# First unit, block barrier and final gate of an attention and feed-forward kernel on one core

## The chip, the cores and the metric

The kernel runs on one core of a Trainium2 chip. A core has a matmul engine (TensorE, PE in the profile; its weight loads are PEld), a vector engine (VectorE, DVE), a scalar engine (ScalarE, ACT), a general engine (GpSimd, POOL) and a queue engine that issues transfers (SyncE, SP). Each works through its own list of instructions in order and waits on semaphores for the others. The metric is the device time of one execution in microseconds (us); lower is better.

## The reference

```python
xn = _layernorm(x)                      # x: (2, 512, 512), float32
s = _L0_attn_ref(xn, wq, wk, wv, wo)    # 32 query heads, 8 key/value heads of 128, RoPE, window 128
g = _silu(_L0_ffn_ref(xn, ...))         # 512 -> 1792 -> 512, weights (int - zero) * scale
x = x + s * g
```

The attention projects `xn` to q, k and v, rotates q and k by position, takes a softmax over the own block of 128 positions and the one before, weighs v with it and projects out with `wo`. The feed-forward part computes `silu(xn @ gate) * (xn @ up)` and multiplies it by `down`.

## The kernel before

There are 1024 tokens, held as 8 tiles of 128. Products are made in three passes of float32r operands: each operand is split into a rounded part (`hi`, a copy on ACT) and a remainder (`lo`, a subtraction on POOL or DVE), and a product is lo·hi + hi·lo + hi·hi (`three_passes`, L36 to L38). A projection of 128 output rows by 512 tokens is 4 × 3 = 12 matmuls.

`attention_block` has one program for each engine. Work is cut into 16 units, one for each pair of key/value head and batch (`unit = 2 * g + b`); a unit has 7 steps that leave PSUM (`PROJ`): k (k = 0), four q (1 to 4), v (5) and the transposed v (6), in three PSUM banks by turns. Each unit has 4 query blocks j. For one block PE transposes the probabilities (`turn_probs`), computes the scores of the next block (`scores`), projects something of the next unit (`project(..., BEFORE[j])`), projects the finished block before out (`project_out`), weighs the values (`weigh_values`), and may project once more (`AFTER[j]`). So the projections of a unit are made while the unit before it is worked on. The first unit (0, 0) has none before it: its projections stand ahead of the loop, after the norm.

`rope` (DVE, L887 on) rotates one projection with four operations: two half-height products with `sin` into a row of `roped`, the product with `cos` in place in PSUM (L894), and their sum into the row (L896), which frees the bank (`proj_drained`). ACT then writes the rounded part (`hi_of_roped`), POOL the remainder (`lo_of_roped`). `roped` has two rows, so the third rotation waits for the first's remainder.

Ahead of the loop DVE computes the statistics of four tiles of x, then their scale by a Newton step (`normed`), then normalises the four tiles; PE transposes them (`turn_x`), ACT and DVE split them (`hi_of_x`, `lo_of_x`). The second four tiles go the same way, with `turn_x(1)` between the projections 2 and 3. POOL writes the remainders of the weights (`weight_lo`) as soon as ACT has written their rounded part. The list of DVE there is, at its end:

```python
            rope(0, 0, 4)
            drain_v(0, 0)
            lo_of_v(0, 0)
            rope(1, 1, 0)
            fold_and_max(0, 0)
            invert(0)
```

The last unit's body already does products of the feed-forward part (`ffn_product`) with the weight tiles that are dequantised beside it: products 0 and 1 (gate and up) in the loop, and product 2 (24 matmuls) after the last `project_out`. Then the block ends: all engines drain and meet at a barrier, and `ffn_block` starts a new program on each. POOL begins it with four memsets of `ffn_acc`, then the remainders of `mid` 0 and 1, then that of weight piece 3 (`fw.lo`), for which PE waits before the second pair's first product.

`ffn_block` runs over 7 pairs of inner tiles. In the end, for each of the 8 token tiles t: PE makes the down product (6 matmuls), DVE adds it to `acc` (`accumulate`, L334), ACT takes silu in place, POOL multiplies by the attention result y (L328), DVE adds x (`join`, L345), SP stores the tile.

Of the kernel before, what the change touches and what calls it, by code (L numbers as in the profile page):

```python
# [12 lines left out]
P = 128  # L13
# [27 lines left out]
class Shared:  # L41
# [6 lines left out]
    def __init__(self, nc, ctx):  # L48
# [20 lines left out]
        self.mid_done = sem("mid_done")  # L69

# [45 lines left out]
EARLY_PRODUCTS = 3  # L116
# [74 lines left out]
def ffn_block(nc, sh, fw, x, out):  # L191
# [4 lines left out]
    with ExitStack() as ctx:  # L196
# [8 lines left out]
        ps_down = ps[:, 4:8, :]  # L205
        silu_done, mid_done = sh.silu_done, sh.mid_done
# [7 lines left out]
        last_gated = sem("last_gated")  # L214
# [21 lines left out]
        def _(sp):  # L236
# [8 lines left out]
            for t in range(TT):  # L245
                sp.wait_ge(joined, t + 1)
                sp.dma_start(out[t * P:(t + 1) * P, :], res[:, t, :]).then_inc(stored, 16)
# [37 lines left out]
        def _(act):  # L285
# [19 lines left out]
            for t in range(TT):  # L305
                act.wait_ge(acc_done, ZEROED + TT * (PAIRS - 1) + t + 1)
                act.activation(acc[:, t, :], acc[:, t, :], ACT.Silu).then_inc(gate_done, 1)

        @block.gpsimd
        def _(pool):  # L310
# [15 lines left out]
            for t in range(TT - 1):  # L326
                pool.wait_ge(gate_done, t + 1)
                pool.tensor_tensor(acc[:, t, :], acc[:, t, :], sh.y[:, t, :], ALU.mult).then_inc(gated, 1)  # L328

        @block.vector  # L330
        def _(dve):
# [4 lines left out]
            def join(t):  # L336
                if t == 0:
                    dve.wait_ge(res_in, 16)
                if t == TT - 1:
                    dve.wait_ge(gate_done, TT)  # L340
                    dve.tensor_tensor(acc[:, t, :], acc[:, t, :], sh.y[:, t, :], ALU.mult).then_inc(last_gated, 1)  # L341
                    dve.wait_ge(last_gated, 1)
                else:
                    dve.wait_ge(gated, t + 1)
                dve.tensor_tensor(res[:, t, :], acc[:, t, :], res[:, t, :], ALU.add).then_inc(joined, 1)  # L345

            def body(n, last):
# [9 lines left out]
                if first(n):  # L357
                    dve.wait_ge(acc_done, ZEROED)
            over_pairs(dve, body)
            for t in range(TT):  # L360
                accumulate(PAIRS, t)
                if t >= 2:
                    join(t - 2)
            for t in range(TT - 2, TT):
                join(t)


def attention_block(nc, sh, fw, x, wq, wk, wv, wo, cos_in, sin_in, causal_in, keep_in, ident_in):
# [7 lines left out]
    roped = sh.work[:, Shared.ROPE_AT:Shared.ROPE_AT + 2, :]  # L376
    xin = y
    PROJ = 7
    TURN = 6
    with ExitStack() as ctx:  # L380
# [46 lines left out]
        xt_done = sem("xt_done")  # L427
        y_zeroed = sem("y_zeroed")
# [24 lines left out]
        y_ready = sem("y_ready")  # L453
# [55 lines left out]
        BEFORE, AFTER = (1, 3, 5), (2, 4, None)  # L509
# [35 lines left out]
        def _(pe):  # L545
# [69 lines left out]
            def ffn_product(e, kind, ks=range(KT)):  # L615

                if ks[0] == 0:
# [6 lines left out]
                    if (e, kind) == (2, GATE):  # L624
                        pe.wait_ge(sh.silu_done, 1)
                    if (e, kind) == (2, UP):
                        pe.wait_ge(sh.mid_done, 1)
                sh.gate_up(pe, e, kind, ks)

            pe.wait_ge(ident_ld, 16)  # L630
# [12 lines left out]
            def body(g, last):  # L643
                for b in range(2):
# [3 lines left out]
                    for j in range(QB):  # L648
# [8 lines left out]
                        if ahead and j < QB - 1:  # L657
                            project(gn, un, bn, BEFORE[j])
# [13 lines left out]
                        if ahead and j < QB - 1 and AFTER[j]:  # L672
                            project(gn, un, bn, AFTER[j])
            over_heads(pe, body)
            project_out(NKV - 1, 1, QB)
            ffn_product(2, GATE)
            ffn_product(2, UP)

        @block.scalar
        def _(act):  # L680
# [3 lines left out]
            def hi_of_roped(unit, b, i):  # L684
                act.wait_ge(proj_drained, unit * PROJ + (i + 1))
                act.activation(rope_target(b, i)[0], roped[:, (5 * b + i) % 2, :], ACT.Copy).then_inc(rope_hi, 1)  # L686
# [37 lines left out]
            for t in range(1, TT, 2):  # L724
                act.dma_start(xin[:, t, :], x[t * P:(t + 1) * P, :]).then_inc(x_in[t], 16)
                if t == GROUP - 1:
                    act.dma_start(ident[:, :], ident_in).then_inc(ident_ld, 16)
            root_of_var(0)
# [5 lines left out]
            root_of_var(1)  # L734

# [305 lines left out]
```

## Time and profile before

| | |
|---|---|
| median of 3 runs | 915.43 us (915.4 to 917.39) |
| profiled execution, its own time | 917.41 us |
| its span, first to last instruction | 915.6 us |
| mean granted TensorE clock | 0.992 |
| PE busy | 881.3 us (96%) |
| DVE busy | 658.6 us (72%) |
| POOL busy | 462.7 us (51%) |
| ACT busy | 449.2 us (49%) |

Busy is the time in which an engine has an instruction under way. Successive matmuls overlap, so that a busy PE can be a full one at either clock; where it waits, a row of the timeline ends with the idle time in front of it and what released it, as `[2.05 <-POOL w_lo L188]`.

### The profile page before, as it was taken

To read this page: it belongs to the slowest core of one execution; us is meant where nothing else is said; L and a number is where in the kernel's file an instruction comes from. 1 tells how busy PE (TensorE), PEld (TensorE's weight loads), DVE (VectorE), ACT (ScalarE), POOL (GpSimd) and SP (SyncE) were. 2 spreads that over 40 slices of the span, in tenths; PEclk is the share of its full clock that TensorE was granted. 3 is DMA by queue.
4 is the path that set the end of the run, shared out by engine and by line. 5 is a ranking of instruction groups with operands and counts; after the bars stand their busy time and mean duration, and the time that the engine had idled before them with its cause. 6 is when DMAs were issued, how large, how long until landed. Compare 5 with 4: busy or idle time off the path is not lost. (4 is left out here: it accounts for less than half of the span.)

```text
span 915.6 us, 14375 instructions
## 1 busy us (share of the span) xinstructions
PE 881.3 (96%) x4384; PEld 744.1 (81%) x4384; DVE 658.6 (72%) x1069; ACT 449.2 (49%) x1240; POOL 462.7 (51%) x358
## 2 busy tenths in 40 slices
PE   4779999999999999999999999999998999999996
PEld 3668888888888888888888888888787888888885
DVE  7767778687777868777787787778665656666656
ACT  3345565655556565555656555564652213213223
POOL 3445555555565555546555554654346435435436
PEclk9989999999999999999999999999999999999998
DMA  8010111101011010101101110002224365446542
GB/s 252 3 55 24 36 39 32 35 24 46 23 34 46 23 34 26 43 23 34 46 23 34 34 34 23 23 24 80 70 70 133 102 179 162 115 135 172 130 169 92
DMA packets 84443, 61.43 MB, mean 67 GB/s; under 512 B 3648, under 2 KB 71616, under 8 KB 84416
## 3 DMA queue, kind: packets, MB, share of 16 engines
q1 hardware_dynamic: 83696, 59.98, 22.4%
q10 hardware_dynamic: 720, 1.11, 0.3%
q8 instruction: 14, 0.23, 0.1%
q14 instruction: 13, 0.11, 0.0%
HBM read 58.98 MB, written 2.10 MB: 67 GB/s over the span
## 5 line engine op out<-in xcount | busy, mean ns | idle before, releaser
L36 PE MATMUL ps<-xt_hi,w_lo 128*128 128x512 f32 x608 | 240.9, 396 | 6.4 <-POOL w_lo L188 2.3
L37 PE MATMUL ps<-xt_lo,w_hi 128*128 128x512 f32 x608 | 239.0, 393 | 0.0
L38 PE MATMUL ps<-xt_hi,w_hi 128*128 128x512 f32 x608 | 238.2, 392 | 0.0
L797 POOL TENSOR_TENSOR q_lo<-work,q_hi 128x512 fp32r<-128x512 f32 x64 | 82.8, 1294 | 174.4 <-ACT q_hi L686 174.4
L802 POOL TENSOR_TENSOR pt_lo<-kept,pt_hi 128x512 fp32r<-128x512 f32 x112 | 143.7, 1302 | 31.0 <-ACT pt_hi L707 31.0
L36 PEld LDWEIGHTS ps<-xt_hi,w_lo 128*128 128x128 f32 x608 | 115.6, 190 | 30.2 <-issue 5.9
L38 PEld LDWEIGHTS ps<-xt_hi,w_hi 128*128 128x128 f32 x608 | 115.3, 190 | 24.7
L37 PEld LDWEIGHTS ps<-xt_lo,w_hi 128*128 128x128 f32 x608 | 115.7, 190 | 21.6
L696 ACT ACTIVATE probs<-ps,neg_max 128x128 f32<-128x128 f32 x256 | 90.7, 367 | 58.4 <-DVE neg_max L909 58.4
L707 ACT ACTIVATE pt_hi<-kept 128x512 fp32r<-128x512 f32 x112 | 69.2, 633 | 68.1 <-DVE kept L919 68.1
L36 PE MATMUL ps<-wo_hi,o_lo 128*128 (+1 forms) x256 | 99.8, 390 | 0.1
L37 PE MATMUL ps<-wo_lo,o_hi 128*128 (+1 forms) x256 | 99.6, 389 | 0.0
L38 PE MATMUL ps<-wo_hi,o_hi 128*128 (+1 forms) x256 | 99.6, 389 | 0.0
L702 ACT ACTIVATE probs<-probs,inv 128x128 f32<-128x128 f32 x256 | 81.6, 390 | 17.1 <-DVE inv L913 17.1
L686 ACT ACTIVATE q_hi<-work 128x512 fp32r<-128x512 f32 x64 | 40.5, 632 | 94.0 <-DVE work L896 94.0
L188 POOL TENSOR_TENSOR w_lo<-work,w_hi 128x512 fp32r<-128x512 f32 x42 | 57.2, 1366 | 56.8 <-ACT w_hi L183 56.8
L919 DVE TENSOR_TENSOR kept<-ps,keep_sb 128x512 f32<-128x512 f32 x112 | 72.5, 683 | 17.1 <-PE ps L577 17.1
L925 DVE TENSOR_TENSOR o_lo<-ps,o_hi 128x512 fp32r<-128x512 f32 x64 | 44.3, 692 | 51.4 <-ACT o_hi L711 51.4
L315 POOL TENSOR_TENSOR mid_lo<-kept,mid_hi 128x512 fp32r<-128x512 f32 x28 | 44.5, 1590 | 65.0 <-ACT mid_hi L292 65.0
L36 PE MATMUL ps<-k_hi,q_lo 128*128 128x256 f32 (+1 forms) x256 | 76.5, 299 | 0.0
L499 POOL TENSOR_TENSOR w_lo<-work,w_hi 128x512 fp32r<-128x512 f32 x48 | 61.8, 1297 | 23.6 <-ACT w_hi L494 23.6
L38 PE MATMUL ps<-k_hi,q_hi 128*128 128x256 f32 (+1 forms) x256 | 72.2, 282 | 0.0
(79 smaller groups left out, 1723.3 us busy)
## 6 DMA issues: line engine op xcount, KB each, us to landing
work<-L_attn_wq SPq DMA_DIRECT2D x32, 256.0 KB, 2.8
work<-L_attn_wo SPq DMA_DIRECT2D x32, 256.0 KB, 2.6
work<-L_ffn_gate_w SPq DMA_DIRECT2D x14, 256.0 KB, 3.2
work<-L_ffn_gate_z SPq DMA_DIRECT2D x14, 256.0 KB, 4.3
work<-L_ffn_gate_s SPq DMA_DIRECT2D x14, 256.0 KB, 5.4
work<-L_ffn_up_w SPq DMA_DIRECT2D x14, 256.0 KB, 3.6
work<-L_ffn_up_z SPq DMA_DIRECT2D x14, 256.0 KB, 4.1
work<-L_ffn_up_s SPq DMA_DIRECT2D x14, 256.0 KB, 4.5
```

The source lines that it names most:

```text
L36: pe.matmul(out, stat[1], mov[0], start=first, stop=False)
L37: pe.matmul(out, stat[0], mov[1], start=False, stop=False)
L38: return pe.matmul(out, stat[0], mov[0], start=False, stop=last)
L188: pool.tensor_tensor(lo, self.sh.dq(at % Shared.DQ), hi.bitcast(F32), ALU.subtract).then_inc(self.sh.w_split, 1)
L315: pool.tensor_tensor(mid_lo[:, ii, cols], mid[:, e % 2, :], mid_hi[:, ii, cols].bitcast(F32), ALU.subtract).then_inc(mid_split, 1)
L499: pool.tensor_tensor(lo, raw[p % RING][:, :], hi.bitcast(F32), ALU.subtract).then_inc(w_split, 1)
L696: act.activation(probs[:, h, :], ps_score[:, h, 1, :], ACT.Exp, bias=neg_max[:, h:h + 1], accum_out=total[:, h:h + 1]).then_inc(exp_done, 1)
L702: act.activation(probs[:, h, :], probs[:, h, :], ACT.Copy, scale=inv[:, h:h + 1]).then_inc(probs_ready, 1)
L707: act.activation(pt_hi[:, w, :], kept[:, w, :], ACT.Copy).then_inc(pt_hi_done, 1)
L797: pool.tensor_tensor(lo, roped[:, (5 * b + i) % 2, :], hi.bitcast(F32), ALU.subtract).then_inc(rope_split, 1)
L802: pool.tensor_tensor(pt_lo[:, w, :], kept[:, w, :], pt_hi[:, w, :].bitcast(F32), ALU.subtract).then_inc(pt_split, 1)
L919: dve.tensor_tensor(kept[:, w, :].rearrange("p (h c) -> p h c", h=GQ), ps_pt.rearrange("p (h c) -> p h c", h=GQ), keep[:, w, :].unsqueeze( ...
```

## The change

It has three parts.

- **First unit.** `rope_first` replaces `rope` for the five rotations of unit (0, 0): DVE makes the two `sin` products into one of four rows and the `cos` product into a second buffer (`direct`), which frees the PSUM bank; POOL adds the two (`sum_of_roped`). PE makes the first projection pass by pass (`project_first`), runs projections 0 to 4 ahead of `turn_x(1)`, and runs projections 0 and 1 of unit (1, 1) ahead of the loop; DVE's `rope(1, 1, 0)` stands behind `invert(0)`. The normalisation of the second four tiles goes from one DVE pass to two ACT passes (`centre`, `scale`). POOL waits for the first four normalised tiles before it starts on the weights; ACT and POOL split the `wo` pieces after the first softmax. In the body, the first unit projects (2, 3, 5) and then (none, 4, none).
- **Barrier.** Product 2 of the feed-forward part is left to `ffn_block` (`EARLY_PRODUCTS` 2), and so is the last addition to y.
- **Final gate.** ACT writes silu to a PSUM bank, DVE multiplies it by y from there (`gate`), and POOL adds x for tiles 0 to 6; DVE does the addition of tile 7.

```diff
-EARLY_PRODUCTS = 3
+EARLY_PRODUCTS = 2
...
-                act.activation(acc[:, t, :], acc[:, t, :], ACT.Silu).then_inc(gate_done, 1)
+                wait(act, gated, t - 3)
+                act.activation(gate_of(t), acc[:, t, :], ACT.Silu).then_inc(gate_done, 1)
...
             for t in range(TT - 1):
-                pool.wait_ge(gate_done, t + 1)
-                pool.tensor_tensor(acc[:, t, :], acc[:, t, :], sh.y[:, t, :], ALU.mult).then_inc(gated, 1)
+                if t == 0:
+                    pool.wait_ge(res_in, 16)
+                pool.wait_ge(gated, t + 1)
+                pool.tensor_tensor(res[:, t, :], acc[:, t, :], res[:, t, :], ALU.add).then_inc(joined, 1)
...
+            def gate(t):
+                dve.wait_ge(gate_done, t + 1)
+                dve.tensor_tensor(acc[:, t, :], gate_of(t), sh.y[:, t, :], ALU.mult).then_inc(gated, 1)
...
+            dve.wait_ge(sh.y_ready, NKV * TT)
+            dve.tensor_tensor(sh.y[:, TT - 1, :], ps[:, 7, :], sh.y[:, TT - 1, :], ALU.add)
             over_pairs(dve, body)
             for t in range(TT):
                 accumulate(PAIRS, t)
-                if t >= 2:
-                    join(t - 2)
-            for t in range(TT - 2, TT):
-                join(t)
+                if t >= 1:
+                    gate(t - 1)
+            gate(TT - 1)
+            dve.wait_ge(res_in, 16)
+            dve.wait_ge(gated, TT)
+            dve.tensor_tensor(res[:, TT - 1, :], acc[:, TT - 1, :], res[:, TT - 1, :], ALU.add).then_inc(last_joined, 1)
...
+            def project_first():
+                cols, out = slice(0, SEQ), bank(0, K_)
+                pe.wait_ge(xt_hi_done, GROUP)
+                pe.wait_ge(xt_done, 1)
+                pe.wait_ge(w_hi_done, 1)
+                for t in range(KT):
+                    pe.matmul(out, w_hi[:, K_, t, :], xt_hi[:, t, cols], start=t == 0, stop=False)
+                pe.wait_ge(w_split, 1)
+                for t in range(KT):
+                    pe.matmul(out, w_lo[:, K_, t, :], xt_hi[:, t, cols], start=False, stop=False)
+                pe.wait_ge(xt_done, GROUP)
+                for t in range(KT):
+                    last = pe.matmul(out, w_hi[:, K_, t, :], xt_lo[:, t, cols], start=False, stop=t == KT - 1)
...
-            pe.wait_ge(xt_done, GROUP)
-            for k in range(TURN):
-                if k == 3:
+            project_first()
+            for k in range(1, TURN):
+                if k == V_:
                     turn_x(1)
                 project(0, 0, 0, k)
+            turn_v(0, 0)
             pe.wait_ge(xt_done, TT)
-            scores(0, 0, 0, 0, range(0, 2))
-            turn_v(0, 0)
+            scores(0, 0, 0, 0)
             project(0, 1, 1, 0)
-            scores(0, 0, 0, 0, range(2, GQ))
+            project(0, 1, 1, 1)
...
             project_out(NKV - 1, 1, QB)
-            ffn_product(2, GATE)
-            ffn_product(2, UP)
...
+            centre(1)
+            hi_of_roped(0, 0, 0)
+            scale(1)
             act.wait_ge(root_done, 2)
             act.activation(preload[:, 0:1], root[:, 0:1], ACT.Exp)
-            hi_of_roped(0, 0, 0)
             hi_of_roped(0, 0, 1)
+            hi_of_roped(0, 0, 2)
             hi_of_x(1)
-            hi_of_roped(0, 0, 2)
             hi_of_roped(0, 0, 3)
+            hi_of_roped(0, 0, 4)
+            act.wait_ge(proj_ready, V_ + 1)
+            act.activation(v_t[:, :], bank(0, V_), ACT.Copy).then_inc(proj_drained, 1)
+            hi_of_v(0, 0)
+            exps(0)
+            normalise(0)
             for p in range(6, 8):
                 weight_hi(act, 0, p)
-            hi_of_roped(0, 0, 4)
-            hi_of_v(0, 0)
+            hi_of_roped(1, 1, 0)
             for p in range(8, 10):
                 weight_hi(act, 0, p)
...
+            pool.wait_ge(xn_done, GROUP)
             for p in range(6):
                 weight_lo(pool, 0, p)
+            sum_of_roped(0)
+            sum_of_roped(1)
             for i in range(5):
                 lo_of_roped(0, 0, i)
-            for p in range(WO_, NPIECE):
+                if i + 2 < 5:
+                    sum_of_roped(i + 2)
+            pool.wait_ge(turned, TT)
+            pool.memset(y[:, TT - 1, :], 0.0).then_inc(y_zeroed, 1)
+            for p in range(WO_, WO_ + 2):
                 weight_lo(pool, 0, p)
             lo_of_roped(1, 1, 0)
+            for p in range(WO_ + 2, NPIECE):
+                weight_lo(pool, 0, p)
...
+            def rope_first(i):
+                half, at = P // 2, bank(0, i)
+                dve.wait_ge(proj_ready, i + 1)
+                wait(dve, rope_split, i - 3)
+                dve.tensor_tensor(roped_first[i % 4][0:half, :], at[half:P, :], sin[half:P, :], ALU.mult).then_inc(sin_done, 1)
+                dve.tensor_tensor(roped_first[i % 4][half:P, :], at[0:half, :], sin[0:half, :], ALU.mult).then_inc(sin_done, 1)
+                wait(dve, rope_sum, i - 1)
+                dve.tensor_tensor(direct[:, i % 2, :], at, cos[:, :], ALU.mult).then_inc(proj_drained, 1)
...
+            rope_first(0)
             normed(1)
-            rope(0, 0, 0)
-            rope(0, 0, 1)
+            for i in range(1, 5):
+                rope_first(i)
             lo_of_x(1)
-            rope(0, 0, 2)
-            rope(0, 0, 3)
-            rope(0, 0, 4)
-            drain_v(0, 0)
             lo_of_v(0, 0)
-            rope(1, 1, 0)
             fold_and_max(0, 0)
             invert(0)
+            rope(1, 1, 0)
```

## Rows read from the trace of the kernel before

**Rows 1.** The page's first part: busy time, share of the span, instructions.

```profile
PE 881.3 (96%) x4384; PEld 744.1 (81%) x4384; DVE 658.6 (72%) x1069; ACT 449.2 (49%) x1240; POOL 462.7 (51%) x358
```

**Rows 2.** Busy time by stage: length, engines, granted clock, DMA share, GB/s.

```profile
80.00:670.00 590.00, 588.84 (x3092) 502.90 (x3091) 448.28 (x782) 348.04 (x1034) 313.04 (x246) 1.00 0.12 36
700.00:880.00 180.00, 180.00 (x790) 148.97 (x789) 113.83 (x132) 45.83 (x79) 82.15 (x57) 0.99 0.55 154
```

**Rows 3.** Who PE waited for: us in total, times, the longest.

```profile
PE ps L612 <- DVE y L868: 10.2, 1, 10.2
PE ps L577 <- ACT probs L702: 6.9, 2, 6.0
PE ps L558 <- DVE v_t L879: 2.7, 1, 2.7
...
PE ps L36 <- DVE work L896: 2.2, 1, 2.2
```

**Rows 4.** Timeline of the first 23 us: start, length, engine, operation.

```profile
8.06 1.25 DVE L863 TENSOR_SCALAR r<-corr 128x4 f32<-128x4 f32 x1
...
9.54 2.87 DVE L868 TENSOR_SCALAR y<-y,mv,rstd 128x512 f32<-128x512 f32 x4
...
14.01 0.60 ACT L721 ACTIVATE xt_hi<-ps 128x512 fp32r<-128x512 f32 x1 [0.26 <-PE ps L612]
...
15.38 0.79 PE L36 MATMUL ps<-xt_hi,w_lo 128*128 128x512 f32 x1 [1.41 <-DVE xt_lo L874]
...
20.85 1.92 DVE L868 TENSOR_SCALAR y<-y,mv,rstd 128x512 f32<-128x512 f32 x4
```

**Rows 5.** Groups of the first 80 us by shape: mean ns behind the bar.

```profile
L797 POOL TENSOR_TENSOR q_lo<-work,q_hi 128x512 fp32r<-128x512 f32 x7 | 9.0, 1291 | 21.2 <-ACT q_hi L686 21.2
L894 DVE TENSOR_TENSOR ps<-ps,tables 128x512 f32<-128x512 f32 x10 | 7.0, 699 | 0.3
...
L686 ACT ACTIVATE q_hi<-work 128x512 fp32r<-128x512 f32 x7 | 4.4, 632 | 14.4 <-DVE work L896 14.4
```

**Rows 6.** Timeline of the first blocks of unit (0, 0), PE and DVE.

```profile
47.83 0.69 DVE L907 TENSOR_TENSOR ps<-ps,causal_sb 128x512 f32<-128x512 f32 x1
...
51.65 1.35 PE L577 MATMUL ps<-ident_sb,probs 128*128 128x128 f32 x4 [6.03 <-ACT probs L702]
...
62.46 0.60 PE L577 MATMUL ps<-ident_sb,probs 128*128 128x128 f32 x4
...
64.34 0.40 PE L36 MATMUL ps<-xt_hi,w_lo 128*128 128x512 f32 x1
...
73.89 0.60 PE L577 MATMUL ps<-ident_sb,probs 128*128 128x128 f32 x4
```

**Rows 7.** Timeline around the barrier, PE and POOL.

```profile
684.93 0.39 PE L38 MATMUL ps<-wo_hi,o_hi 128*128 128x512 f32 x1
...
691.05 3.64 POOL L324 MEMSET ffn_acc<- 128x1024 f32 x4 [10.06 <-POOLq L380]
...
691.24 0.47 PE L36 MATMUL ps<-xt_hi,w_lo 128*128 128x512 f32 x1 [0.48 <-PEq L380]
...
696.55 0.39 PE L38 MATMUL ps<-xt_hi,w_hi 128*128 128x512 f32 x1
698.99 0.77 PE L36 MATMUL ps<-xt_hi,w_lo 128*128 128x512 f32 x1 [2.05 <-POOL w_lo L188]
...
702.50 0.40 PE L38 MATMUL ps<-xt_hi,w_hi 128*128 128x512 f32 x1
```

**Rows 8.** The end: two rows of the timeline, two of the lines L345 and L328 (ns min/median/max).

```profile
907.22 0.39 PE L38 MATMUL ps<-w_hi,mid_hi 128*128 128x512 f32 x1
...
912.47 0.69 DVE L345 TENSOR_TENSOR res<-ffn_acc,res 128x512 f32<-128x512 f32 x1
...
L345 DVE TENSOR_TENSOR res<-ffn_acc,res x8: 678/1164/1306, 901.5 to 912.5; 128x512 f32<-128x512 f32 x8
...
L328 POOL TENSOR_TENSOR ffn_acc<-ffn_acc,y x7: 1294/1493/1635, 899.6 to 909.2; 128x512 f32<-128x512 f32 x7
```

More of the change, by code:

```diff
@@ L376, in attention_block @@
     roped = sh.work[:, Shared.ROPE_AT:Shared.ROPE_AT + 2, :]
+    roped_first = [sh.work[:, Shared.ROPE_AT + row, :] for row in (0, 1, -4, -3)]
+    direct = sh.work[:, Shared.ROPE_AT - 2:Shared.ROPE_AT, :]
     xin = y
@@ L506, in attention_block, with row_of, before, after @@
         FFN_AT = {(0, 3): (-2,), (1, 0): (-1,), (1, 1): (0,), (1, 2): (1,), (1, 3): (2,)}
-        BEFORE, AFTER = (1, 3, 5), (2, 4, None)
+        def row_of(unit, b, i):
+            return roped_first[i % 4] if isinstance(unit, int) and unit == 0 else roped[:, (5 * b + i) % 2, :]
+        def before(g, b, j):
+            return ((2, 3, 5) if first_unit(g, b) else (1, 3, 5))[j]
+        def after(g, b, j):
+            return ((None, 4, None) if first_unit(g, b) else (2, 4, None))[j]
+        def left(g, b, j):
+            return ((1, None, 4) if first_unit(g, b) else (None, 2, 4))[j]
+        def first_unit(g, b):
+            return isinstance(g, int) and (g, b) == (0, 0)
         BANK = ((0, 1, 2, 0, 1, 2, 0), (1, 2, 0, 1, 2, 0, 1))
@@ L657, in body @@
                         if ahead and j < QB - 1:
-                            project(gn, un, bn, BEFORE[j])
+                            project(gn, un, bn, before(g, b, j))
                         elif not last:
@@ L671, in body @@
                             ffn_product(1, UP, range(2, KT))
-                        if ahead and j < QB - 1 and AFTER[j]:
-                            project(gn, un, bn, AFTER[j])
+                        if ahead and j < QB - 1 and after(g, b, j):
+                            project(gn, un, bn, after(g, b, j))
             over_heads(pe, body)
             project_out(NKV - 1, 1, QB)
-            ffn_product(2, GATE)
-            ffn_product(2, UP)
         @block.scalar
@@ L684, in hi_of_roped @@
             def hi_of_roped(unit, b, i):
[L685 to L686 removed]
+                if isinstance(unit, int) and unit == 0:
+                    act.wait_ge(rope_sum, i + 1)
+                else:
+                    act.wait_ge(proj_drained, unit * PROJ + (i + 1))
+                act.activation(rope_target(b, i)[0], row_of(unit, b, i), ACT.Copy).then_inc(rope_hi, 1)
             def hi_of_v(unit, b):
@@ L727, in _, with centre, scale @@
                     act.dma_start(ident[:, :], ident_in).then_inc(ident_ld, 16)
+            def centre(group):
+                for t in range(group * GROUP, (group + 1) * GROUP):
+                    act.activation(xin[:, t, :], xin[:, t, :], ACT.Identity, scale=-1.0, bias=mv[:, t, 0:1]).then_inc(centred, 1)
+            def scale(group):
+                act.wait_ge(newton, 5 * (group + 1))
+                for t in range(group * GROUP, (group + 1) * GROUP):
+                    act.wait_ge(centred, t - group * GROUP + 1)
+                    act.activation(xin[:, t, :], xin[:, t, :], ACT.Copy, scale=rstd[:, t:t + 1]).then_inc(xn_done, 1)
             root_of_var(0)
@@ L763, in body @@
                             exps(n + 1)
-                        if ahead and 0 < j < QB - 1:
-                            hi_of_roped(un, bn, AFTER[j - 1])
+                        if ahead and j < QB - 1 and left(g, b, j):
+                            hi_of_roped(un, bn, left(g, b, j))
                         if ahead and j == QB - 1:
@@ L822, in body @@
                         lo_of_probs(unit, j)
-                        if ahead and 0 < j < QB - 1:
-                            lo_of_roped(un, bn, AFTER[j - 1])
+                        if ahead and j < QB - 1 and left(g, b, j):
+                            lo_of_roped(un, bn, left(g, b, j))
                         if ahead and j < 2:
-                            lo_of_roped(un, bn, BEFORE[j])
+                            lo_of_roped(un, bn, before(g, b, j))
                         if not last and j == QB - 1:
@@ L971, in body @@
                             fold_and_max(n + 1, (j + 1) % QB)
-                        if ahead and 0 < j < QB - 1:
-                            rope(un, bn, AFTER[j - 1])
+                        if ahead and j < QB - 1 and left(g, b, j):
+                            rope(un, bn, left(g, b, j))
                         if ahead and j == QB - 1:
```

51 lines of the change are left out of this document (23 added, 28 removed).

## Prediction

> **What bounds the kernel now.** First the page's busy times: PE is busy in 96% of the span, DVE in 72%, POOL in 51% [rows 1]. The stages say where the missing 4% lies. In the 590 us of the loop over heads PE is busy for 588.8, and in the 180 us of the feed-forward loop for all 180, with the clock at 1.00 and 0.99 [rows 2]. No edit there is worth anything, and this change makes none. What can be won stands in three places: ahead of the loop, at the barrier, behind the last matmul. The list of what PE waited for names them: 10.2 us until the first normalised tile, 6.9 for the softmax (6.0 of it in one wait), 2.7 for the drained v, 2.2 for a rotation [rows 3]. What the barrier costs shows only in the timeline [rows 7], and so does the end [rows 8].
>
> The unit of PE's time: 24 matmuls of 128x512 start between 691.24 and 696.55, 23 steps in 5.31 us, 0.23 each; eight steps from 698.99 to 702.50 take 3.51, 0.44 each [rows 7]. The first is TensorE at 2.4 GHz, the second mostly at 1.2. A projection of 12 matmuls is 2.75 us.
>
> **First unit, up to the first projection.** A Newton step on 4 elements took 1.25 us while POOL wrote a weight's remainder [rows 4]; the other such steps are short, as can be seen from the room of 1.5 us between its start and that of the normalisation. The four normalising passes took 2.87 us beside POOL and 1.92 in the second group, without it [rows 4]. With POOL held back until they are done, the step ends 1.1 us earlier, and the passes start at 8.45 for 9.54. PE's first transposes come 1.1 us earlier (9.1 for 10.2), the last rounded tile, which ended at 14.6 (14.01 + 0.60), at about 13.45: 1.1 earlier, a little for the one wait on a slow pass that goes. `project_first` needs only that and the first remainder, where `project` waited for the fourth remainder until 15.38 [rows 4]. So the first projection starts at 13.55, 1.8 us earlier. POOL's weights come later (first remainder at 11.7, ready before PE's second pass at 15.3), and with it the transfer of the v weight that waits for this remainder; it is used five projections later. I price both at nothing; without that cover they cost up to the 2.4 us of their delay.
>
> The clock is at its lower level here and I let it stay there for as long after the first transposes as before. Projection 0 then takes 12 x 0.44 = 5.3 and ends at 18.9.
>
> **First unit, rotations.** A rotation was 4 DVE operations of some 0.7; now it is 3 on DVE (2.2 us with their gaps) and one on POOL, at POOL's 1.29 for the same tile, where it already wrote each remainder, 1.29 too [rows 5]. The trace has no such sum on POOL; the subtraction L797 is the same kind, shape and memory and I take it. Walk: rotation 0 leaves DVE at 21.3; the Newton steps of the second group stand behind it, one of them blocked by POOL's sum as in [rows 4] (1.3, and 0.8 for the rest), 23.4; rotation 1 leaves at 25.6. From there POOL has 4 sums and 5 remainders in its list, 9 x 1.29 = 11.6: 37.3. PE makes projections 1 to 4 until 29.9 (4 x 2.75), transposes, and makes v until 34.6; DVE needs 2.2 for each rotation and is never later than PE; ACT's eight passes of 0.63 for `centre` and `scale` [rows 5] lie between 18 and 26 and PE wants their tiles at 29.9. So POOL sets the first scores. Before, its share was 5 remainders, and DVE's 4-operation rotation set the pace.
>
> Head 3 of the scores ends at 38.0. From the start of the mask to the first transposed probabilities took 3.8 us (47.83 to 51.65) [rows 6]; all four heads are normalised at about 42.9, the first at 42.0. Meanwhile PE has two projections, 5.5 us, until 43.5. The wait of 6.03 us [rows 6] is gone.
>
> **First unit, the first two blocks.** Here a new wait takes its place. Behind the softmax ACT first writes a `wo` piece (0.63 after 42.9), and POOL has five operations in front of the first `lo_of_probs` (2 wo, k of the next unit, 2 wo): 43.5 + 6 x 1.29 = 51.2. PE has only transposes, scores (62.46 to 64.34, 1.9 us [rows 6]) and one projection, 2.75: it wants the probabilities at 48.1 and waits 3.0. On DVE two rotations of 2.9 and the mask stand in the same stretch; the inverse comes at about 50, and the second probabilities at 51 to 52, just behind. Then `weigh_values` (3 matmuls, 0.7) and block 1, whose work on PE is that of before: 62.46 to 73.89, 11.4 us [rows 6]. PE starts block 2 at 51.2 + 0.7 + 11.4 = 63.3, where it did at 73.89: **10.6 us** earlier. Behind that, the loop is PE's and keeps it.
>
> From this goes the clock. A wait of 2.05 us was followed by 3.5 us at the lower level, which cost 3.51 - 8 x 0.23 = 1.7 [rows 7]; the wait of 2.2 us [rows 3] was not. A wait of 3.0 is longer than both; I take the fall, once: **-1.7**. The other end is nothing.
>
> The Trainium skill speaks against the sums on POOL: "GPSIMD Engine Reference", section 4.1, gives elementwise work on a tile to VectorE, because GpSimd is about twice slower with two inputs. The rows agree: 1.29 to 0.70, 1.85 times. By the page's measured ratio of 1.96 an operation would be 1.37, an estimate, and 15 of them in the chain 1.2 us more; the gain of this part would be 7.7 for 8.9.
>
> **Barrier.** Before, the last `project_out` has its last matmul at 684.93, product 2 follows, PE drains, and the engines restart at 691.05 to 691.24 [rows 7]. PE's restart comes 0.5 behind the end of its last matmul. Without product 2, that matmul ends at 685.3 and PE restarts at 685.8, POOL at 685.6. PE then has product 2 and product 3, 48 x 0.23 = 11.0: 696.8, only 0.2 behind 696.55. But POOL's list (memsets 3.64 [rows 7], two remainders of `mid`, that of piece 3) ended 7.9 after its restart, at about 698.9, and made PE wait 2.05; now it ends at 693.5, covered by 3.3 us. DVE's moved addition (0.7) stands in front of piece 3's dequantisation; POOL is busy until 691.8 anyway. Pieces 4 and 5 are ready by 697.1 and 700.5, where PE wants them at 699.5 and 702.2, so 1.7 us is the thinnest cover. The matmul that stood at 702.50 behind the wait and the slow clock stands at 696.8 + 8 x 0.23 = 698.6: **3.9 us**.
>
> **Final gate.** PE ends the same: last matmul at 907.22 [rows 8], product tiles 1.36 us apart. Before, DVE's `join` read two SBUF tensors and took 1.16 in the middle, 0.68 when alone, POOL's product 1.49 [rows 8]: 0.6 + 1.1 = 1.7 for each tile, and DVE ended at 913.16. Now DVE has two operations from PSUM, 0.7 each, and keeps PE's pace; POOL's 1.29 fits too. From 907.65: addition, silu on ACT 0.66, gate 0.7: 909.75; the last addition reads SBUF beside POOL's addition for tile 6, 0.7 to 1.2: 910.5 to 910.95. The store behind it is unchanged. **2.4 us**, between 2.2 and 2.7. That ACT writes PSUM has no row at this place; SBUF costs it 0.63 [rows 5], I take the same.
>
> **Sum.** 10.6 - 1.7 + 3.9 + 2.4 = 15.2. The span goes from 915.6 to 900.4, the profiled execution's own time from 917.4 to 902.2, the median of the runs, 0.2 below the span, from 915.4 to **900.2**.
>
> **Rivals.**
> - *The clock holds* over the wait in block 0. For it: the waits of 2.7 and 2.2 us [rows 3]. Against: 2.05 sufficed once. 16.9 us, 898.5. Chance 0.23.
> - *POOL is slower.* Its operations beside DVE's two-SBUF ones took up to 1.64 [rows 8]. 15 in the chain at 0.35 more are 5.2 us: 905.4. Against: DVE's rotations read PSUM, and beside them POOL stayed at 1.29 [rows 5]. This is where the page's rule points. Chance 0.17.
> - *The barrier's gain doesn't come*: piece 5 or its transfer is late and PE waits anyway. 904.1. For it: the cover of 1.7. Chance 0.06.
> - *Not faster.* The sums make POOL the bound of the first unit so far that nothing is left. It decides where an operation in the chain takes 1.29 + 15.2 / 15 = 2.3 us; no row of POOL at this shape comes near. At 2.6: 920. Chance 0.03.
> - *Forecast*: 0.51, own range 898.9 to 903.
>
> Range 896 to 906: the low end takes the clock's hold and POOL's chain better hidden (up to the whole wait of 3.0), the high end the slower POOL. 0.3% (2.7 us) is about what a measurement of this kernel tells from no change. Faster 0.95, within 0.3% 0.03, slower 0.02.
>
> **What would show it.** First matmul of projection 0 at about 13.6; POOL gapless from 25.6 to 37; no wait for ACT's probabilities at the first `turn_probs`; one of some 3 us for `pt_lo` in front of the first `weigh_values`, and matmuls at twice their spacing behind it; `turn_probs` of block 2 at 63. PE's list of waits without `w_lo` behind the barrier, restart near 675 in the new time. DVE's operations at the end at 0.7, the last one 3 us behind the last matmul. I am wrong if ACT, which has 8 passes more and a table load, holds the rotations' rounded parts back, or if the second projection finds no weights since POOL started on them late.

## The result and the profile after

The changed kernel takes 899.81 us in the median (899.41 to 900.3), the kernel before beside it 916.18 (915.4 to 917.39); the ratio is 0.982 (95% interval 0.9803 to 0.9837). Forecast were 900.2 us and a range of 896 to 906. The profiled execution's span went from 915.6 to 898.1 us, 17.5 shorter.

The page after, its first two parts (span, busy time, and the granted clock in tenths):

```profile
span 898.1 us, 14371 instructions
...
PE 876.7 (98%) x4384; PEld 740.6 (82%) x4384; DVE 648.1 (72%) x1059; ACT 454.7 (51%) x1249; POOL 467.2 (52%) x363
...
PEclk9999999999999999999999999999999999999999
```

What PE waited for, after:

```profile
PE ps L640 <- DVE y L940: 9.1, 1, 9.1
PE ps L36 <- POOL pt_lo L858: 2.7, 1, 2.7
PE ps L586 <- ACT v_t L799: 1.0, 1, 1.0
PE ps L605 <- ACT probs L743: 0.9, 1, 0.9
...
PE ps L36 <- POOL w_lo L189: 0.5, 2, 0.3
```

Against [rows 3]: the first tile comes 1.1 us earlier, the softmax's 6.9 is 0.9, the drained v's 2.7 is 1.0, and in their place stands one new wait, for `pt_lo`.

The timeline of the first unit after, PE and POOL:

```profile
9.14 3.65 PE L640 MATMUL ps<-ident_sb,y 128*128 128x128 f32 x16 [9.14 <-DVE y L940]
...
13.48 2.07 PE L661 MATMUL ps<-xt_hi,w_hi 128*128 128x512 f32 x4 [0.69 <-ACT xt_hi L762]
...
25.02 1.30 POOL L864 TENSOR_TENSOR work<-work 128x512 f32<-128x512 f32 x1 [2.73 <-DVE work L966]
...
33.75 2.51 POOL L853 TENSOR_TENSOR q_lo<-work,q_hi 128x512 fp32r<-128x512 f32 x2
...
42.29 0.60 PE L605 MATMUL ps<-ident_sb,probs 128*128 128x128 f32 x4
...
48.31 1.28 POOL L858 TENSOR_TENSOR pt_lo<-kept,pt_hi 128x512 fp32r<-128x512 f32 x1
...
49.73 0.47 PE L36 MATMUL ps<-pt_hi,v_lo 128*128 128x512 f32 x1 [2.68 <-POOL pt_lo L858]
...
50.50 0.60 PE L605 MATMUL ps<-ident_sb,probs 128*128 128x128 f32 x4
...
61.92 0.60 PE L605 MATMUL ps<-ident_sb,probs 128*128 128x128 f32 x4
```

POOL works without a gap from 25.02 to 36.2, two operations in 2.51. The last row is block 2, which stood at 73.89 [rows 6]: 11.97 us earlier. Block 1 takes 11.42 us (50.50 to 61.92), as before, and the granted clock from 50 to 62 us is 1.00: TensorE stayed at the upper of its two levels (2.4 GHz, matmuls of 512 columns 0.23 us apart; at the lower, 1.2 GHz, they are 0.43 apart) behind the wait.

Around the barrier, after:

```profile
672.99 0.39 PE L38 MATMUL ps<-wo_hi,o_hi 128*128 128x512 f32 x1
...
673.66 3.64 POOL L331 MEMSET ffn_acc<- 128x1024 f32 x4 [4.66 <-POOLq L390]
...
673.85 0.47 PE L36 MATMUL ps<-xt_hi,w_lo 128*128 128x512 f32 x1 [0.48 <-PEq L390]
...
679.76 1.29 POOL L189 TENSOR_TENSOR w_lo<-work,w_hi 128x512 fp32r<-128x512 f32 x1
```

and the end, with two of its rows from the timeline and the lines of gate and addition (ns min/median/max):

```profile
891.89 0.39 PE L38 MATMUL ps<-w_hi,mid_hi 128*128 128x512 f32 x1
...
894.46 1.03 DVE L372 TENSOR_TENSOR res<-ffn_acc,res 128x512 f32<-128x512 f32 x1
...
L347 DVE TENSOR_TENSOR ffn_acc<-ps,y x8: 678/680/691, 884.8 to 893.7; 128x512 f32<-128x512 f32 x8
...
L337 POOL TENSOR_TENSOR res<-ffn_acc,res x7: 1264/1292/1303, 885.6 to 893.7; 128x512 f32<-128x512 f32 x7
```

From the last `project_out` to the last matmul PE needs 891.89 - 672.99 = 218.9 us, where it was 907.22 - 684.93 = 222.3 [rows 7, 8]: 3.4 less. From the last matmul's start to DVE's end it is 3.6 for 5.9 (912.47 + 0.69 - 907.22). So the span's 17.5 are 11.9 in front of the barrier, 3.4 behind it, 2.3 at the end, less 0.1 to 0.2 in the last store. It is more than the 16.4 between the medians, since the profiled execution before (917.41) was a long one for its kernel (median 916.18) and the one after (900.3) lies 0.5 above its median.

### The profile page after: what moved, and what is told of

Read it like the earlier page. It is cut to its first block and busy times, and to the rows that moved or that the text cites. A ratio compares the mean times of both kernels' runs of the same rounds, so it can differ in the third digit from the quotient of the medians.

```text
span 898.1 us, 14371 instructions
## 1 busy us (share of the span) xinstructions
PE 876.7 (98%) x4384; PEld 740.6 (82%) x4384; DVE 648.1 (72%) x1059; ACT 454.7 (51%) x1249; POOL 467.2 (52%) x363
## 5 line engine op out<-in xcount | busy, mean ns | idle before, releaser
L36 PE MATMUL ps<-xt_hi,w_lo 128*128 128x512 f32 x604 | 236.8, 392 | 0.7 <-PEq L390 0.5
L37 PE MATMUL ps<-xt_lo,w_hi 128*128 128x512 f32 x604 | 235.6, 390 | 0.0
L38 PE MATMUL ps<-xt_hi,w_hi 128*128 128x512 f32 x604 | 235.1, 389 | 0.0
L38 PEld LDWEIGHTS ps<-xt_hi,w_hi 128*128 128x128 f32 x604 | 113.4, 188 | 23.9
L36 PEld LDWEIGHTS ps<-xt_hi,w_lo 128*128 128x128 f32 x604 | 113.6, 188 | 23.1 <-issue 0.9
L37 PEld LDWEIGHTS ps<-xt_lo,w_hi 128*128 128x128 f32 x604 | 113.7, 188 | 21.3
L511 POOL TENSOR_TENSOR w_lo<-work,w_hi 128x512 fp32r<-128x512 f32 x48 | 61.6, 1296 | 23.7 <-ACT w_hi L506 13.7
```

The costliest lines, as they stand in the source:

```text
L36: pe.matmul(out, stat[1], mov[0], start=first, stop=False)
L37: pe.matmul(out, stat[0], mov[1], start=False, stop=False)
L38: return pe.matmul(out, stat[0], mov[0], start=False, stop=last)
L511: pool.tensor_tensor(lo, raw[p % RING][:, :], hi.bitcast(F32), ALU.subtract).then_inc(w_split, 1)
```

## The experiments

Three kernels have one part of the change each; eight start from the changed kernel; one is the changed kernel again. A ratio is to the kernel before in the same series. The second number column is the profiled execution's span.

| run | median us (before) | ratio, 95% interval | span |
|---|---|---|---|
| first unit alone | 905.79 (916.72) | 0.9886 (0.987 to 0.9903) | 901.9 |
| barrier alone | 913.6 (916.72) | 0.9964 (0.9952 to 0.9976) | 912.0 |
| final gate alone | 914.64 (916.72) | 0.998 (0.997 to 0.9989) | 911.7 |
| POOL at once | 900.85 (916.3) | 0.9828 (0.9811 to 0.9844) | 899.4 |
| sums on DVE | 901.48 (916.3) | 0.9838 (0.9822 to 0.9854) | 899.2 |
| wo pieces behind | 900.4 (916.3) | 0.9822 (0.9803 to 0.9842) | 898.5 |
| both waits | 901.28 (916.3) | 0.9843 (0.9824 to 0.9863) | 898.5 |
| changed kernel again | 900.33 (915.78) | 0.9825 (0.9811 to 0.9838) | 897.3 |
| one projection ahead | 904.11 (915.78) | 0.9864 (0.9849 to 0.9879) | 902.9 |
| rotation first | 904.93 (915.78) | 0.9874 (0.9859 to 0.9889) | 903.7 |
| longer wait | 902.69 (915.78) | 0.9856 (0.9841 to 0.9872) | 899.6 |
| gate from SBUF | 904.46 (915.75) | 0.9876 (0.9859 to 0.9893) | 902.2 |

### The parts alone

Each is the kernel before with one part of the diff ahead of the prediction, and the others left as they were. The first has all hunks of `project_first`, `first_unit`, `sum_of_roped` and the lists of the first blocks. The second has only this (with the calls and waits of product 2 gone from `attention_block`, and `add_y` moved behind the barrier as in the diff):

```diff
-EARLY_PRODUCTS = 3
+EARLY_PRODUCTS = 2
```

and the third only the end: ACT writes the silu into PSUM, DVE multiplies it with `y`, POOL adds.

> Only the first unit's part of the change; barrier and final gate as before. Theory (the three parts add up, and all that the first unit wins is kept): the span is 12.0 us shorter than that of before (block 2's transposes at 61.9 instead of 73.9), about 903.6, and the wait behind the barrier is again some 2 us with the slow matmuls behind it. Rival (the parts lean on each other: the shift moves the load of weights behind the barrier against the products): the wait there grows or goes, and the gain is under 11 or over 13.

> Only the barrier's part: product 2 and the last addition to y behind the barrier. Theory: 3.4 to 3.9 us shorter than before, span 911.7 to 912.2, made up of the 2.05 us wait, 1.7 of slow clock, 0.1 of the rest. Rival (part of the gain in the changed kernel came from the shift of the transfers by the first unit's gain): under 2.5 us.

> Only the final gate's part. Theory: 2.2 to 2.4 us shorter than before, span 913.3; DVE's operations at 0.69 at PE's pace of 1.36 us a tile. Rival (the end is the store's, whose transfers queue up behind a late first one): under 1 us, with the last store landing as late as before.

By the medians they win 10.4, 3.3 and 1.8 us (one less the ratio, times 916), together 15.5, where the whole wins 16.0 to 16.5: they add up within what is measured. The profiles are sharper. From the last `project_out` to the last matmul the old barrier takes 221.3 us with the first unit alone (672.19 to 893.48) and 221.5 with the gate alone (684.12 to 905.59); the new one takes 218.4 with the barrier alone (685.21 to 903.60). That is 3.0 us, and not the 3.9 of the forecast. The rows in the gate's run that answer to the wait of 2.05 [rows 7]:

```profile
698.18 0.49 PE L36 MATMUL ps<-xt_hi,w_lo 128*128 128x512 f32 x1 [2.02 <-POOL w_lo L188]
701.50 0.50 PE L36 MATMUL ps<-xt_hi,w_lo 128*128 128x512 f32 x1 [0.31 <-POOL w_lo L188]
```

The same wait, and this time the clock stayed up (0.49 where it was 0.77); then a second wait of 0.31 shows, which the slow matmuls had covered. The first unit alone shows the same pair, 2.06 and 0.31. The 1.7 us of slow clock that I had put into the barrier's account belonged to that one execution, which took 0.8 to 1.0 longer here (222.3) than these two.

The end's 5.9 and 3.6 us are the same in all three (5.93, 5.93, 3.60): 2.3 us.

All three rivals fell: the parts add up, the barrier alone wins over 2.5 us, the gate over 1. But two of the three spans miss what was expected, since each compares one execution with one other. With the first unit alone the span is 13.7 us shorter for 12.0: block 2 starts 12.75 earlier (61.14), with the first projection at the upper level of the clock, and 1.0 is the clock behind the barrier. With the gate alone it is 3.9 shorter for 2.2 to 2.4: 2.3 at the end, 0.8 at the barrier and 0.8 ahead of the loop. The barrier's 3.6 fits its 3.4 to 3.9, but with the slow matmuls of the profile before in it.

### The changed kernel again

> The changed kernel itself once more, to see how far its own clock varies from one execution to another. Theory (when the clock goes up and down depends on where in the execution the chip happens to look, not on the kernel's edit): the profiled execution may have projection 0 at either level and may lose 1.5 us behind the 2.7 us wait, which the first profile did not; the waits themselves, in us, are those of the first profile within 0.1 where the clock in front of them is the same. Rival (the level is fixed by the kernel's instructions): the same levels at the same places.

The timeline of PE at the places of the first unit:

```profile
9.28 3.65 PE L640 MATMUL ps<-ident_sb,y 128*128 128x128 f32 x16 [9.28 <-DVE y L940]
13.62 1.19 PE L661 MATMUL ps<-xt_hi,w_hi 128*128 128x512 f32 x4 [0.69 <-ACT xt_hi L762]
...
34.03 0.66 PE L586 MATMUL ps<-ident_sb,v_t 128*128 128x128 f32 x4 [2.03 <-ACT v_t L799]
...
41.36 0.60 PE L605 MATMUL ps<-ident_sb,probs 128*128 128x128 f32 x4
...
48.76 0.47 PE L36 MATMUL ps<-pt_hi,v_lo 128*128 128x512 f32 x1 [2.62 <-POOL pt_lo L858]
49.53 0.60 PE L605 MATMUL ps<-ident_sb,probs 128*128 128x128 f32 x4
60.96 0.60 PE L605 MATMUL ps<-ident_sb,probs 128*128 128x128 f32 x4
```

The same program, but projection 0 runs at the upper level's pace from its first matmul (4 in 1.19 us for 2.07; the granted clock reads 1.00 from 9 to 22 us in both profiles, so that here only the spacing tells the level). PE is 2 us ahead when it transposes the second tiles, then waits 1.0 more for v, which ACT copies only behind POOL's chain; 0.96 us is left at block 2. So the clock early in the kernel is worth less than its own time, since POOL sets the pace there. Of the 11 profiles with `project_first`, 8 show projection 0 at the upper level and 3 at the lower. The wait for `pt_lo`, the same 2.6 to 2.7 us in six of them, was followed by slow matmuls in three (POOL at once, sums on DVE, gate from SBUF) and not in the other three. Where it was, block 1 took 12.95 to 12.97 us for 11.4, and the granted clock from 50 to 62 us was 0.86 for 1.00; the spacing doubled only 1 to 1.5 us behind the end of the wait. So these levels vary with the execution: projection 0 in two profiles of the same program, the fall behind the wait between this program and "gate from SBUF", which differs from it only at the end. What decides it in an execution no run shows. Comparisons below take profiles at the same levels where they can.

### POOL's hold and POOL's sums

> The changed kernel, but POOL starts on the weights at once instead of waiting for the first four normalised tiles. Theory (POOL's two-input operations block DVE's small steps and slow its passes): the first transposes start at 10.2 instead of 9.14, a DVE step of 1.25 us comes back, and the whole is 1.0 us longer, up to 1.4 if the clock rises later too. Rival (the start is bound by other things, such as the transfer of wq): no more than 0.3 us longer.

```diff
-            pool.wait_ge(xn_done, GROUP)
```

> The changed kernel with four rows, but the first unit's sums on DVE again, four operations for each rotation. Theory (POOL's chain of 9 operations from 25.0 to 36.2 and DVE's rotations are nearly in balance): DVE then needs 2.9 us for each of rotations 1 to 4, 22.9 to 34.5, and 2.5 for the remainders of x behind them, so that the scores start at 37 instead of 35.4: 1.5 to 2.5 us longer than the changed kernel. Rival (GpSimd is the dearer place, and freeing it of 5 operations wins): 1 us or more shorter.

```diff
-                wait(dve, rope_sum, i - 1)
-                dve.tensor_tensor(direct[:, i % 2, :], at, cos[:, :], ALU.mult).then_inc(proj_drained, 1)
+                dve.wait_ge(sin_done, 2 * i + 2)
+                dve.tensor_tensor(at, at, cos[:, :], ALU.mult).then_inc(cos_first, 1)
+                dve.wait_ge(cos_first, i + 1)
+                dve.tensor_tensor(roped_first[i % 4], at, roped_first[i % 4], ALU.add).then_inc(proj_drained, 1)
```

(`sum_of_roped` and its calls go; ACT waits for `proj_drained` again.) PE's timeline, first with POOL at once, then with the sums on DVE:

```profile
10.27 3.74 PE L640 MATMUL ps<-ident_sb,y 128*128 128x128 f32 x16 [10.27 <-DVE y L939]
...
50.87 0.60 PE L605 MATMUL ps<-ident_sb,probs 128*128 128x128 f32 x4
```

```profile
33.83 0.66 PE L586 MATMUL ps<-ident_sb,v_t 128*128 128x128 f32 x4 [1.94 <-ACT v_t L796]
35.07 0.33 PE L36 MATMUL ps<-k_hi,q_lo 128*128 128x128 f32 x1 [0.59 <-DVE xt_lo L934]
...
50.17 0.60 PE L605 MATMUL ps<-ident_sb,probs 128*128 128x128 f32 x4
```

Both had projection 0 at the upper level, as the changed kernel again, whose block 1 starts at 49.53. POOL at once starts it 1.34 us later, as expected (in the medians 0.5, less than they can tell). Its DVE step of 1.25 us is back, under POOL's first remainder at 8.05. But whether the step is blocked depends on when the first piece of the weights arrives. The gate's run has no hold either, and there the piece came later (DVE, ACT, PE and POOL):

```profile
8.08 0.17 DVE L865 TENSOR_SCALAR r<-corr 128x4 f32<-128x4 f32 x1
...
8.76 0.63 ACT L496 ACTIVATE w_hi<-work 128x512 fp32r<-128x512 f32 x1 [1.32 <-DMA work<-L_attn_wk]
...
9.17 3.65 PE L614 MATMUL ps<-ident_sb,y 128*128 128x128 f32 x16 [9.17 <-DVE y L870]
...
9.47 3.01 POOL L501 TENSOR_TENSOR w_lo<-work,w_hi 128x512 fp32r<-128x512 f32 x2 [9.02 <-ACT w_hi L496]
```

So the hold buys 1.1 us in three of the four profiles without it (10.23 to 10.30) and nothing in this one; all ten with it start at 9.05 to 9.28. It makes the early start certain.

The sums on DVE start block 1 0.64 later (0.77 if counted from projection 0): in the direction of the theory, at a third to a half of its size, and the medians' intervals overlap. Before the scores PE then waits 0.59 for the remainder of x, which DVE reaches late, where it waits for nothing with the sums on POOL. So moving the sums is worth 0.6 to 0.8 us in this pair. The two engines are nearly in balance; most of this part's gain is made elsewhere.

### The order around the first softmax

> The changed kernel without projection 1 of unit (1, 1) ahead of the loop; the first unit's blocks project (1, 3, 5) and (2, 4, none) as all others. Theory (the second projection fills the softmax's 4 us): PE waits some 2.7 us more for the first probabilities, block 1 starts 2.7 us later, and the whole is 2.5 to 3 us longer than the changed kernel. Rival (POOL's list sets the first block anyway, and the projection is made in its shadow at either place): under 1 us longer.

```diff
-            return ((2, 3, 5) if first_unit(g, b) else (1, 3, 5))[j]
+            return (1, 3, 5)[j]
...
-            project(0, 1, 1, 1)
```

(the two other lists of projections lose their first unit's case in the same way.)

> The changed kernel with DVE's rotation of (1, 1, 0) back ahead of the first mask and maximum. Theory: the mask waits for projection (1, 1, 0) and 2.9 us of rotation and starts at about 42.5 instead of 37.0, the first probabilities come at 46.5 for 42.3, and all behind follows: 4 us longer. Rival (the projections ahead already cover it): under 1.5 us.

```diff
             lo_of_v(0, 0)
+            rope(1, 1, 0)
             fold_and_max(0, 0)
             invert(0)
-            rope(1, 1, 0)
```

PE's timeline with one projection ahead, then with the rotation first:

```profile
40.62 1.20 PE L605 MATMUL ps<-ident_sb,probs 128*128 128x128 f32 x4 [0.93 <-ACT probs L742]
...
49.67 0.77 PE L36 MATMUL ps<-pt_hi,v_lo 128*128 128x512 f32 x1 [3.66 <-POOL pt_lo L857]
...
55.92 0.60 PE L605 MATMUL ps<-ident_sb,probs 128*128 128x128 f32 x4
```

```profile
46.76 1.35 PE L605 MATMUL ps<-ident_sb,probs 128*128 128x128 f32 x4 [3.75 <-ACT probs L743]
...
55.81 0.47 PE L36 MATMUL ps<-pt_hi,v_lo 128*128 128x512 f32 x1 [1.29 <-POOL pt_lo L858]
```

With one projection ahead the wait for `pt_lo` ends at the same time (49.67 for 49.73), but projection 2 is still to be made behind it, at the lower clock: block 1 starts at 55.92, 5.4 later than in the first profile of the changed kernel with its equal start. Of that 2.7 is the projection and the rest the clock, whose granted level was 0.50 from 50 to 54 us: behind the wait of 3.66 us 14 matmuls start 0.43 apart and not 0.23. The medians say 3.8. With the rotation first the probabilities come at 46.8 for 41.4, block 1 at 56.6 for 49.5 with the lower level in two stretches, and the medians say 4.6. Both rivals fell. The rotation's theory held, in its times and near its 4 us; that of the projection held only in direction: the wait for the first probabilities is 0.93 and not 2.7 longer, that for `pt_lo` 1.0 longer, and the cost, above the 2.5 to 3 expected, is the projection made behind it. Each of the two costs some 4 us when it alone is taken back, so that they matter more than the sums; how much they win together, and what the four rows, the order of the projections, `project_first` and ACT's two passes win, no run shows apart.

### The new wait

> The changed kernel with one subtraction of 1.25 us more in POOL's list ahead of the first block's probabilities (wo piece 9 is subtracted twice). Theory: the wait for pt_lo grows from 2.7 to 3.9 us and the whole is 1.2 us longer, plus up to 1.6 where the clock falls in it, so 1.2 to 2.8. Rival (another engine holds the first block back as well, so POOL has slack): under 0.6 us.

```diff
-            for p in range(WO_ + 2, NPIECE):
-                weight_lo(pool, 0, p)
+            weight_lo(pool, 0, WO_ + 2)
+            pool.wait_ge(w_hi_done, NPIECE)
+            hi, lo = split_target(0, NPIECE - 1)
+            for i in range(1):
+                pool.tensor_tensor(lo, raw[4][:, :], hi.bitcast(F32), ALU.subtract).then_inc(repeated, 1)
+                pool.wait_ge(repeated, i + 1)
+            weight_lo(pool, 0, NPIECE - 1)
```

> The changed kernel with the four wo pieces of the first unit behind the first block's probabilities, on ACT and on POOL. Theory (POOL's list makes the 2.68 us wait, but DVE's rotation between the mask and the inverse is the next one, 0.85 behind): the wait for pt_lo goes, one of 1.5 to 2.0 for the second probabilities comes in its place, and the whole is 0.5 to 1.0 us shorter. Rival (the POOL list is all): 2.5 us shorter.

```diff
-            for p in range(WO_, WO_ + 2):
-                weight_lo(pool, 0, p)
...
-            for p in range(WO_ + 2, NPIECE):
-                weight_lo(pool, 0, p)
...
                         lo_of_probs(unit, j)
+                        if first_block(g, b, j):
+                            for p in range(WO_, WO_ + 2):
+                                weight_lo(pool, 0, p)
```

(the other two pieces go behind the rotation of this block, and ACT's list follows in the same way.)

> As the kernel before, and in the first block the inverse and the normalisation stand ahead of the rotation of projection 1. Theory: both waits go, 2.3 to 2.7 us shorter than the changed kernel. Rival (the rotations are then late for projection 3 or for the remainder of o): under 1.5 us, with a new wait of PE for DVE's rotation or for o_lo.

```diff
                         fold_and_max(n + 1, (j + 1) % QB)
+                        if first_block(g, b, j):
+                            invert(n + 1)
                         if ahead and j < QB - 1 and left(g, b, j):
                             rope(un, bn, left(g, b, j))
...
-                        if more:
+                        if more and not first_block(g, b, j):
                             invert(n + 1)
```

(on DVE; ACT's `normalise(n + 1)` moves in the same way. "The kernel before" in this expectation is the one with the wo pieces behind.)

The longer wait is 3.98 us in its profile and costs 2.4 us in the medians (902.69 for 900.33), inside the 1.2 to 2.8 of the theory: POOL's list has no slack there. In the profile the clock fell with it (the first matmul behind the wait takes 0.64 for 0.47). With the wo pieces behind:

```profile
49.22 1.21 PE L608 MATMUL ps<-ident_sb,probs 128*128 128x128 f32 x4 [1.94 <-ACT probs L746]
62.85 0.60 PE L608 MATMUL ps<-ident_sb,probs 128*128 128x128 f32 x4
```

The wait for `pt_lo` is gone and one of 1.94 for the second probabilities has taken its place, as expected; block 1 starts 1.28 earlier (49.22 for 50.50, same level at projection 0). The 1.21 us for the four transposes, 0.60 elsewhere, is not the clock, which was granted at 1.00 until 51 us: they follow ACT, which normalises the four heads in 1.26 us. Then, from 51 to 54.3, the clock fell (granted 0.53), and block 2 comes at 62.85, 0.9 later. The medians show no difference, so the expected 0.5 to 1.0 us was not seen. With both waits taken away:

```profile
47.49 1.20 PE L608 MATMUL ps<-ident_sb,probs 128*128 128x128 f32 x4 [0.28 <-ACT probs L746]
54.82 0.47 PE L36 MATMUL ps<-wo_hi,o_lo 128*128 128x512 f32 x1 [1.94 <-DVE o_lo L1016]
58.30 0.47 PE L36 MATMUL ps<-pt_hi,v_lo 128*128 128x512 f32 x1 [0.49 <-POOL pt_lo L865]
```

Block 1 starts 2.04 us earlier than in the changed kernel again, and more than that is lost: PE waits 1.94 for the remainder of o and 0.7 for those of the next probabilities (0.49 and another 0.21), and its four transposes take 0.6 longer at ACT's pace. Block 2 starts at 62.97 for 60.96. The clock has no part in it, it is granted at 1.00 from 9 to 63 us. The chain in front of the remainder of o is DVE's second rotation (until 52.8), ACT's rounded part of it and then of o (52.83 to 53.95), DVE's subtraction (53.98). The rival held: DVE's two rotations of 2.9 in this block are the floor under the POOL wait. Neither version beats the changed kernel.

### The final gate

> The changed kernel, but ACT writes the final silu in place in acc (SBUF), so that DVE's gate reads two SBUF tensors beside POOL's addition; who does what is as in the change. Theory (what wins is that DVE's operation doesn't share its second SBUF input with POOL): the gate takes 1.1 to 1.2 us instead of 0.69, a tile on DVE 1.7 instead of 1.36, and the end comes 1.5 to 2.3 us later behind the last matmul, 5.1 to 5.9 for 3.6. Rival (what wins is that DVE has the product and POOL the addition, and the last tile's one operation less in a row): under 0.5 us later.

```diff
-        gate_of = lambda t: ps[:, t % 4, :]
+        gate_of = lambda t: acc[:, t, :]
```

```profile
L347 DVE TENSOR_TENSOR ffn_acc<-ffn_acc,y x8: 680/1367/1398, 885.2 to 897.3; 128x512 f32<-128x512 f32 x8
...
898.09 1.56 DVE L372 TENSOR_TENSOR res<-ffn_acc,res 128x512 f32<-128x512 f32 x1
```

The gate takes 1.37 us beside POOL's addition for 0.68, and the last operation 1.56 for 1.03. From the last matmul (892.30) to DVE's end it is 7.35 us for 3.60: 3.75 later, more than the 1.5 to 2.3 of the theory, since in the median each takes about as long as POOL's beside it (1.37 against 1.29), as if the two engines took turns. The medians say 4.1 (904.46 for 900.33). The rival fell. Giving the product to DVE and the addition to POOL is worse than the kernel before (5.9) without the bank of PSUM; the bank is the whole gain and more. "GPSIMD Engine Reference" of the Trainium skill, section 8, names contention with VectorE instructions that have two SBUF inputs; the runs agree and give it a size, 0.68 against 1.37.

## Why the prediction was right, and where its terms were off

- **Start.** PE's first transpose 9.14 (9.1 forecast), projection 0 at 13.48 (13.55), the v weight's later transfer hidden. Right. That projection 0 runs at the lower level was so in this profile and in 2 of the 10 others with `project_first`.
- **Rotations.** POOL's chain of 9 sets the scores, from 25.0 to 36.2 for 25.6 to 37.3; its operations follow each other at 1.25, not 1.29. The step holds, but its reason was too broad: the sums alone are worth 0.6 to 0.8 us, the order and the second projection some 4 us each when taken back alone.
- **First blocks.** New wait of 2.68 for 3.0, at 49.7 for 51.2; block 1's 11.4 exactly. The gain until block 2 is 11.97 us where 10.6 stood. Of the 1.4, 1.0 is the chain, which started 0.6 sooner and ran 0.4 quicker; the six operations behind the softmax are 0.2 shorter.
- **Clock.** This is the term that was mis-sized: "-1.7", and it was 0 in the first profile. I took a level for a consequence of the wait's length. Over six profiles with that wait it fell in three, where block 1 took 1.5 longer, so the term is 0 or 1.5, by the execution. What the first profile and the changed kernel again show is the rival "the clock holds".
- **Barrier.** 3.9 forecast, 3.4 measured between the two first profiles, 3.0 at equal clock. For the execution that it was read from the 3.9 was right (222.3 against the 218.3 to 218.4 of the ten other profiles with the new barrier); 0.9 of it was that execution's slow clock, not offset by the wait that it covered. The first profile after takes 218.9, with one more wait of 0.3 for `w_lo` at 723. The covers behind the barrier held: PE waits there for nothing.
- **Final gate.** 2.4 forecast, 2.3 measured.
- **From span to median.** The sum took the new median to lie 0.2 us below the span, as 915.43 lies below 915.6. That was the distance of one long execution (917.41) from the median of three. After, the median of 899.81 lies 1.7 above the span of 898.1, and the kernel before has medians of 915.8 to 916.7 in the later series. This step was wrong by 1.9 us.

So the forecast of the span, 900.4, was 2.3 too high (too little gain: 1.4 to block 2 and 1.7 of clock; too much: 0.5 at the barrier, and some 0.2 at the end), and the step to the median took 1.9 off again. That the sum came within 0.4 us of the median is luck; the places, the new wait and the sizes of the gate and of the start were not.

## What to carry to other kernels

Rows that follow a wait show the clock of that execution; before they enter a sum, see whether the same wait in another profile was followed by the same level, or carry it as two values. A long operation alone does not show it: four transposes of 1.20 us for 0.60 stood at a granted clock of 1.00, because their inputs came one by one. A profiled execution has its own distance from the median (2.0 us above it before, 0.5 after), so a forecast made from its span needs that distance as a term of its own. When a stretch in front of a loop is spread over four engines, move the order and what PE can do ahead first, then single operations: here the first gave some 4 us each and the second 0.6 to 0.8. Two engines that both read two SBUF tensors slow each other down to turns (0.68 to 1.37 here); one operand in PSUM keeps them apart.

## What was not expected of the hardware

- Projection 0 follows nothing but 16 transposes, and in 8 of 11 profiles its matmuls ran at the upper level from the first one (4 in 1.19 us, at 13.62 in the changed kernel again), in 3 at the lower (4 in 2.07, at 13.48). The 16 transposes start at the lower level (median 421 ns each, where the second group's take 272), and in three profiles (rotation first, longer wait, gate from SBUF) the last of them are down to 272 or 273 ns, before any other matmul. "TensorE: Matmul & The Clock Gate" of the Trainium skill, Part 4, says that the full clock does not engage for transposes; these rows don't agree, and the measurement decides.
- The length of a wait doesn't tell what the clock does behind it: of six waits of 2.6 to 2.7 us, three were followed by the lower level and three were not; one of 1.94 was, 2 us behind its end (wo pieces behind), and one of 2.05 at the barrier, but not those of 2.02 and 2.06 at the same place. What the chip counts can't be read from these rows; it stays open.
- DVE's operation of two SBUF tensors beside POOL doubles (0.68 to 1.37), but the same operation with one operand in PSUM stays at 0.68, and POOL at 1.29, in every tile.
